# Down products with both weight parts as one moving operand of 512 columns, centred output weights, and one slot for both attention halves

## The reference

```python
def attention(h):                            # 8 heads of 32, norm_w of 32
    q, k, v = h @ Wq.T, h @ Wk.T, h @ Wv.T
    o = causal linear attention, in chunks of 64:
        inter = q @ state; intra = (q k^T * tril) @ v; state += k^T v
    denom = max(|sum(q * cumsum(k))|, 1)
    o = o / denom
    o = o * rsqrt(mean(o * o) + 1e-5) * norm_w
    return o @ Wo.T

def ffn(h):                                  # 8 experts, 256 -> 256 -> 256, all of them computed
    w = routing weights of 8 experts from sigmoid(h @ Wr / temperature)
    e_out = (silu(h @ Wg[e]) * (h @ Wu[e])) @ Wd[e]
    return sum over e of w[e] * e_out

x = x + _layernorm(attention(_layernorm(x)))
x = x + _layernorm(ffn(_layernorm(x)))
```

## Time and profile before

| | |
|---|---|
| median of 3 runs | 1494.8 us (1493.81 to 1496.97) |
| the profiled execution | 1496.2 us |
| its span | 1494.5 us |
| mean granted clock of PE | 0.995 of full |
| PE busy | 98% |
| DVE busy | 69% |
| ACT busy | 43% |
| POOL busy | 30% |
| DMA | 24.6 MB, 16 GB/s over the span |

### The profile page before, as it was taken

One profiled execution on the slowest core, in us unless ns is written; L12 is line 12 of the kernel. 1 busy time (PEld: TensorE's weight loads), 2 busy tenths in 40 slices (PEclk: granted clock), 3 DMA queues, 4 the chain that ended last, 5 costly groups with the idle time before them and its releaser, 6 DMA issues. The chain is left out here.

```text
span 1494.5 us, 37390 instructions
## 1 busy us (share of the span) xinstructions
PE 1465.5 (98%) x14438; PEld 1279.1 (86%) x14438; DVE 1023.8 (69%) x2492; ACT 647.2 (43%) x1189; POOL 442.9 (30%) x653
## 2 busy tenths in 40 slices
PE   7799999999999999999999999999999999999997
PEld 6688888888888888888888888888888888888886
DVE  6667667676776767667675776767667676776765
ACT  5443534445354443534445354443534445344333
POOL 1403414133251233414134141232413234141231
PEclk9899999999999999999999999999999999999999
DMA  5100000000000000000000000000000000000000
GB/s 171 57 2 15 15 0 14 14 14 14 0 18 10 14 14 9 19 0 14 14 14 14 0 14 14 14 14 0 28 0 14 14 14 14 0 14 16 2 8 22
DMA packets 25345, 24.59 MB, mean 16 GB/s; under 512 B 2016, under 2 KB 25056, under 8 KB 25312
## 3 DMA queue, kind: packets, MB, share of 16 engines
q1 hardware_dynamic: 25312, 24.13, 5.1%
HBM read 15.74 MB, written 8.39 MB: 16 GB/s over the span
## 5 line engine op out<-in xcount | busy, mean ns | idle before, releaser
L1002 DVE TENSOR_TENSOR late<-late,up_ps 128x512 f32<-128x512 f32 x256 | 174.9, 683 | 155.7 <-PE up_ps L436 99.1
L705 ACT ACTIVATE h_hi<-late 128x512 fp32r<-128x512 f32 x256 | 161.6, 631 | 247.2 <-DVE late L1002 247.2
L436 PE MATMUL down_ps<-w_hi,h_hi 128*128 128x256 f32 x976 | 264.5, 293 | 0.0
L786 ACT ACTIVATE late<-gate_ps 128x512 f32<-128x512 f32 x256 | 152.3, 595 | 252.1 <-PE gate_ps L436 252.1
L436 PE MATMUL down_ps<-w_hi,h_lo 128*128 128x256 f32 x976 | 254.1, 282 | 0.0
L1225 POOL TENSOR_TENSOR rms_in<-rms_in,minus_half 128x16 f32<-128x16 f32 x32 | 93.4, 2919 | 498.3 <-DVE rms_in L958 498.3
L899 DVE TENSOR_TENSOR h_lo<-late,h_hi 128x512 fp32r<-128x512 f32 x256 | 175.7, 686 | 65.0 <-ACT h_hi L705 65.0
L1024 DVE SCALAR_TENSOR_TENSOR late<-down_ps,route,late 128x256 f32<-128x256 f32 x364 | 158.4, 477 | 87.9 <-PE down_ps L436 84.9
L436 PE MATMUL gate_ps<-ft_hi,w_hi 128*128 128x512 f32 x512 | 204.9, 400 | 1.0 <-ACT ft_hi L705 0.8
L436 PE MATMUL gate_ps<-ft_hi,w_lo 128*128 128x512 f32 x512 | 203.5, 397 | 0.0
L436 PE MATMUL up_ps<-ft_hi,w_hi 128*128 128x512 f32 x512 | 199.7, 390 | 0.0
(11 more groups left out here) (170 smaller groups left out, 2481.9 us busy)
## 6 DMA issues: line engine op xcount, KB each, us to landing
xs<-in_x SPq DMA_DIRECT2D x32, 256.0 KB, 2.9
out_rows<-late SPq DMA_DIRECT2D x32, 256.0 KB, 2.2
late<-in_wg SPq DMA_DIRECT2D x7, 256.0 KB, 4.1
late<-in_wu SPq DMA_DIRECT2D x7, 256.0 KB, 4.4
late<-in_wd SPq DMA_DIRECT2D x6, 256.0 KB, 4.2
late<-in_wkv_t SPq DMA_DIRECT2D x1, 512.0 KB, 3.9
x<-in_wd SPq DMA_DIRECT2D x2, 256.0 KB, 4.6
late<-in_wq_t SPq DMA_DIRECT2D x1, 256.0 KB, 4.6
```

Of the source, the lines that this page charges most:

```text
L436: last = nc.tensor.matmul(dst, lhs, rhs, start=n == 0, stop=n == len(terms + low_terms) - 1)
L705: return nc.scalar.activation(dst, src, ACT.Copy)
L786: nc.scalar.activation(h_f[:, m, :], gate_ps[:, :], ACT.Silu).then_inc(silu_ready[0], 1)
L1002: nc.vector.tensor_tensor(h_f[:, m, :], h_f[:, m, :], up_ps[m][:, :], ALU.mult).then_inc(h_ready[0], 1)
```

## The change

What is computed stays the same up to the order of sums.

1. **Down products.** `w_hi` and `w_lo` become two halves of one tensor `w_parts`. A tile of `h_hi` meets both parts of the down weights in one matmul of 512 moving columns; the result has high-part products in columns 0 to 255 and low-part products in 256 to 511. A tile of `h_lo` meets the high part only, into columns 0 to 255. Each token tile now has a bank of its own (`down_ps` has two), and `acc` has 512 columns a tile. `add_down` adds all 512; for expert 7 a further `tensor_tensor` adds the two halves into `fin`. ACT's copy of expert 0's product and its scaling by the route are twice as long too.
2. **One up bank.** `up_ps` is one bank, so `up(e, m)` waits for the `hidden` just before it, not for the one before that.
3. **Centred output weights.** In the first block each row of the scaled `wo` has its mean subtracted, so the wo product has mean zero. ACT's copy to `rows` and DVE's centring go; DVE takes the moments straight out of PSUM, and `ln2_add` reads PSUM.
4. **Slots.** Both halves of `ot`, of `wo` and of `ln2_stats` stand together, and all of that stands later (below). The normalisation of half 1 before `ft` goes from ACT to DVE (`ln3_norm`), and `ft` waits for both halves before it begins.
5. **State updates.** Two `scalar_tensor_tensor` on all 128 partitions, masked by `odd_even`, in place of four `tensor_tensor` on 32 partitions, for each of four chunks; the state is laid out anew.
6. **Memory and start.** Half 1 of `kz` lies in `x1` (ACT then waits for `x1_copied`), `late` grows from 3072 to 4096 columns, so that no weight unit is staged in `x1`, and the first block's lists are ordered a little differently.
7. **End.** DVE centres the last pair, and multiplies and adds it itself, without ACT.

The rows that follow are the order of instructions, word for word, as the two programs issue them; they hold no times. First DVE in the last pass of `rest`, experts 6 and 7, before: `late<-down_ps` is `add_down`, `late<-late,up_ps` is `hidden`, `x<-...` is `ln2_add` (x is x1), `h_lo` is `low_hidden`.

The diff, cut to its core:

```diff
-    [("ot", 0)],
+    [],
     [("norm_apply", 1), ("carry",)],
-    [("wo", 0), ("ot", 1)],
-    [("ln2_stats", 0)],
-    [("wo", 1), ("ln2_add", 0)],
-    [("ln2_stats", 1)],
-    [("ln3_stats", 0)],
-    [("ln2_add", 1), ("ln3_stats", 1)],
-    [("ln3_apply", 0)],
-    [("ln3_apply", 1)],
+    [("ot", 0), ("ot", 1)],
+    [],
+    [("wo", 0), ("wo", 1)],
+    [("ln2_stats", 0), ("ln2_stats", 1)],
+    [("ln2_add", 0)],
+    [("ln2_add", 1), ("ln3_stats", 0)],
+    [("ln3_stats", 1)],
+    [("ln3_apply", 0), ("ln3_norm", 1)],
...
-        w_hi = sb("w_hi", [P, 3 * E, 2, 256], f32r)
-        w_lo = sb("w_lo", [P, 3 * E, 2, 256], f32r)
+
+        w_parts = sb("w_parts", [P, 2, 3 * E, 2, 256], f32r)
+        w_hi, w_lo = w_parts[:, 0, :, :, :], w_parts[:, 1, :, :, :]
...
-        up_ps = [bank(f"up_ps{m}") for m in range(MT)]
-        down_ps = bank("down_ps")
+        up_ps = bank("up_ps")
+        down_ps = ctx.enter_context(nc.psum_tensor("down_ps", [P, 2, 512], f32))
...
-                reach(pe, h_ready, f, 2 * e + m - 1)
-                into(up_ps[m], 1).then_inc(up_done[0], 1)
+                reach(pe, h_ready, f, 2 * e + m)
+                into(up_ps, 1).then_inc(up_done[0], 1)
...
                 dst = down_bank(e, p, f)
                 for t in range(2):
                     c = slice((2 * p + t) * P, (2 * p + t) * P + P)
-                    last = products(dst[:, t * HID:t * HID + HID],
-                                    [((h_hi[:, e % 2, m, c], h_lo[:, e % 2, m, c]),
-                                      (w_hi[:, 3 * e + 2, m, :], w_lo[:, 3 * e + 2, m, :])) for m in range(MT)])
+                    for m in range(MT):
+                        nc.tensor.matmul(dst[:, t, :], h_hi[:, e % 2, m, c], w_parts[:, :, 3 * e + 2, m, :],
+                                         start=m == 0, stop=False)
+                        last = nc.tensor.matmul(dst[:, t, 0:HID], h_lo[:, e % 2, m, c], w_hi[:, 3 * e + 2, m, :],
+                                                start=False, stop=m == MT - 1)
...
-                    reach(pe, x1n_ready, a, p + 1)
+                    reach(pe, x1n_ready, a, p + 1 if is_first(a) else 2)
...
+                    if step[1] == 1:
+                        reach(act, x1_copied, a, 0)
...
-                elif kind == "wo":
-                    p = step[1]
-                    copy(rows[:, 2 * p:2 * p + 2, :], src)\
-                        .then_inc(wo_copied[0], 1)
...
-                        added = att_half(step, a)[:, i, :].rearrange("p (b g y v) -> p b g y v", b=B, g=HG, y=2)
-                        for j in range(HPG):
-                            x, y = divmod(j, 2)
-                            rows_j = slice(D * j, D * j + D)
-                            before_i, after_i = (state[rows_j, :, m, :, y * VA:(y + 1) * VA] for m in (n + i, n + i + 1))
-                            last = nc.vector.tensor_tensor(after_i, before_i, added[rows_j, :, :, y, :], ALU.add)
+                        added = att_half(step, a)[:, i, :].rearrange("p (n y v) -> p n y v", n=B * HG, y=2)
+                        for y in range(2):
+                            before_i, after_i = (state[:, m, :, :, y * VA:(y + 1) * VA]
+                                                 .rearrange("p b g v -> p (b g) v") for m in (n + i, n + i + 1))
+                            last = nc.vector.scalar_tensor_tensor(after_i, added[:, :, y, :], odd_even[:, y:y + 1], before_i,
+                                                                  ALU.mult, ALU.add)
...
                 elif kind == "ln2_stats":
                     p = step[1]
-                    reach(dve, wo_copied, a, p + 1)
-                    ln_stats(2, rows, range(2 * p, 2 * p + 2), bn2, mv2)
-                    reach(dve, moments_ready[1], a, p + 1)
-
+                    reach(dve, att_done, a, number_of(("wo", p), a) + 1)
+                    for b in range(B):
+                        last = nc.vector.bn_stats(bn2[:, 2 * p + b, :], att_half(("wo", p), a)[:, b, :])
+                    settle(last)
                     for t in range(2 * p, 2 * p + 2):
-                        last = nc.vector.tensor_scalar(rows[:, t, :], rows[:, t, :], mv2[:, t, 0:1], None, ALU.subtract)
-                    last.then_inc(centred[0], 1)
+                        last = nc.vector.bn_aggr(mv2[:, t, :], bn2[:, t, :])
+                    last.then_inc(moments_ready[1][0], 1)
                 elif kind == "ln2_add":
                     p = step[1]
                     reach(dve, rstd_ready[1], a, p + 1)
-                    reach(dve, centred, a, p + 1)
                     reach(dve, x1_copied, a, 0)
-                    for t in range(2 * p, 2 * p + 2):
-                        last = nc.vector.scalar_tensor_tensor(x1[:, t, :], rows[:, t, :], rstd2[:, t:t + 1], xs[:, t, :],
-                                                              ALU.mult, ALU.add)
+
+                    for b in range(B):
+                        t = 2 * p + b
+                        last = nc.vector.scalar_tensor_tensor(x1[:, t, :], att_half(("wo", p), a)[:, b, :], rstd2[:, t:t + 1],
+                                                              xs[:, t, :], ALU.mult, ALU.add)
                     last.then_inc(x1_ready[0], 1)
                 elif kind == "ln3_stats":
                     p = step[1]
                     reach(dve, x1_ready, a, p + 1)
                     ln_stats(3, x1, range(2 * p, 2 * p + 2), bn3, mv3)
+                elif kind == "ln3_norm":
+                    p = step[1]
+                    reach(dve, rstd_ready[2], a, p + 1)
+                    reach(dve, moments_ready[2], a, p + 1)
+                    for t in range(2 * p, 2 * p + 2):
+                        last = nc.vector.tensor_scalar(rows[:, t, :], x1[:, t, :], mv3[:, t, 0:1], rstd3[:, t:t + 1],
+                                                       ALU.subtract, ALU.mult)
+                    last.then_inc(x1n_ready[0], 1)
...
-                    t, src = 2 * p + n, down_bank(e, p, f)[:, n * HID:(n + 1) * HID]
-                    dst = fin if e == E - 1 else acc
-                    last = nc.vector.scalar_tensor_tensor(dst[:, t, :], src, route[:, t, e:e + 1], acc[:, t, :],
-                                                          ALU.mult, ALU.add)
+                    t = 2 * p + n
+                    last = nc.vector.scalar_tensor_tensor(acc[:, t, :], down_bank(e, p, f)[:, n, :], route[:, t, e:e + 1],
+                                                          acc[:, t, :], ALU.mult, ALU.add)
+                if e == E - 1:
+                    settle(last)
+                    ts = slice(2 * p, 2 * p + 2)
+                    last = nc.vector.tensor_tensor(fin[:, ts, :], acc[:, ts, 0:HID], acc[:, ts, HID:2 * HID], ALU.add)
...
+                    for g in range(HG):
+                        last = nc.vector.bn_stats(bn4[:, g, :], wo_raw[:, g, :])
+                    settle(last)
+                    for g in range(HG):
+                        last = nc.vector.bn_aggr(mv4[:, g, :], bn4[:, g, :])
+                    settle(last)
+                    for g in range(HG):
+                        last = nc.vector.tensor_scalar(wo_raw[:, g, :], wo_raw[:, g, :], mv4[:, g, 0:1], None, ALU.subtract)
                     last.then_inc(wo_scaled, 1)
...
+            dve.wait_ge(moments_ready[3][0], 2 * BLOCKS)
+            for t in range(2, 4):
+                last = nc.vector.tensor_scalar(fin[:, t, :], fin[:, t, :], mv4[:, t, 0:1], None, ALU.subtract)
+            settle(last)
+            out_add(nc.vector, dve, 0, f)
+            dve.wait_ge(x1_copied[0], BLOCKS)
+            dve.wait_ge(rstd_ready[3][0], 2 * BLOCKS)
+            for t in range(2, 4):
+                last = nc.vector.scalar_tensor_tensor(x1_kept[:, t, :], fin[:, t, :], rstd4[:, t:t + 1], x1_kept[:, t, :],
+                                                      ALU.mult, ALU.add)
+            last.then_inc(last_out_ready, 1)
 
```

92 lines of the change are left out of this document (46 added, 46 removed).

## The result

The changed kernel takes 1539.6 us (median of 4 runs, 1538.2 to 1542.0) against 1495.4 us before: 1.0297 times as long, 95% interval 1.028 to 1.0315. That is 44 us more; the forecast was 28 us more (1523, range 1508 to 1548). The profiled execution took 1539.0 us with a span of 1537.3, 42.8 us more than before.

What follows compares the result with a forecast made beforehand. PE's order of work was taken as the whole bound. 15 blocks at +2.84 - 0.34 - 0.58 = +1.92 us give +28.8; last block -0.6, ends -0.5: +27.7 on 1494.8, so 1523 us, range 1508 to 1548.

Steps and rivals of the forecast that it cites:

- rival 3: DVE's long additions cost two pairs: +0.75 us a block, 1534 us; chance 0.09 together with rival 4.
- rival 4: Down products: the two-piece moving operand saves nothing, 1532 us; chance 0.09 together with rival 3.
- rival 1: PE's clock also falls around `ft`: 1527 to 1538 us in some blocks, 1549 to 1574 in all; chance 0.17.
- The chain before `ft`: DVE's layer-norm chain makes PE stand 2.84 us a block: 0.8 before expert 6's down product, 2.0 before `ft`.
- POOL's way: Before `ft`: POOL's roots, then normalisation, end at 782.0 on the forecast's clock, together with DVE's way at 782.1.
- The down products: On PE, fewer, wider matmuls save 0.036 us a product, 0.58 us a block, 9.2 us in all.
- A turn: One turn of the loop takes 92.0 us after the change, against 90.1 before.
- The last block: Its products were to take 0.6 us less.
- Rival 5: The single up bank stops PE, `up` waiting for the hidden product; part of the same 2.8 us; no chance of its own.
- Start: First block: wo's copy and centring leave the chain to `ft`, about 1.5 us; with the end -0.5, bounds -4 and +3.
- End: Longer additions and joining the halves outlast the last ACT pass and its waits by about 1 us.

Runs made afterwards that it cites:

- last_block: Changed kernel with one DVE step moved in the last block: hidden product of expert 2, half 0, ahead of the routing weights and scaling; 1542.2 us in its one run.
- order_only: Kernel before with only the new step order in front of `ft`; short additions, centring and two up banks kept; 1530.4 us, ratio 1.0237.
- short_additions: Changed kernel with `add_down` over the first 256 of its 512 columns, low-part sum left out of the output; 1512.5 us, ratio 1.0118.
- one_piece: Changed kernel with the down products' 512-column moving operand taken from one piece, low-part products left out of the output; 1543.5 us in its one run.
- chain_early: Changed kernel, all operations kept, with the slots of the whole chain before `ft` moved earlier; 1506.2 us, ratio 1.0078.
- narrow_down: Kernel of old_order with each down product as 12 matmuls of 256 columns in place of 4 of 512 and 4 of 256; 1513.9 us, ratio 1.0112.
- old_order: Changed kernel with the old step order before `ft`, so with ACT's wo copies and ACT's normalisation of half 1 back; 1511.3 us, ratio 1.011.
- wo_slot_early: Changed kernel with only the start changed: high and low part of the output weights made before the first expert weights; 1542.1 us, ratio 1.0307.
- centred_swap: Kernel before with output weights centred once, no loop centring, and their scaling moved behind low wq and the second normalisation; 1494.7 us, ratio 0.9994.
- centred_warm: Kernel before with output weights centred once, no loop centring, their scaling later, and filler matmuls before `ft` and the first gate; 1497.9 us, ratio 1.0011.

## Why the prediction was right, and what it mis-sized

The direction, the place and the mechanism were right; the size was 16 us short. The standing of PE was sized well; the other large terms all missed to the same side. That the result still lies in the range is in part luck: the high end of 1548 stood for rivals 3, 4 and 1, and none of them came.

- *The chain before `ft`* (2.84 us of standing a block): 0.75 + 1.70 us idle, and 0.91 + 1.86 = 2.77 us when read from the start of one matmul to the next less a usual pitch. Its links (addition pair 1.33, low part 0.60, statistics 1.06) stood as laid. POOL's way, said to end together with DVE's, did not: its last root ended at 799.67 us, and `ln3_norm` began at 800.34, behind DVE's own work. DVE's order alone decided.
- *The down products* (0.58 us a block): this term was mis-sized. A down product that follows other matmuls without a pause takes 1.432 us before and 1.400 after, 0.032 us less and near the forecast's 0.036. But over all of them (239 in the loop of each) it is 1.478 and 1.460, 0.29 us a block. Products whose first matmul is slow in both kernels save less (1.527 to 1.513), and two of the sixteen have a slow first matmul (0.33 us in the place of 0.23) in the changed kernel alone; one of them is the product that waits for `h_lo`. Inside the down products a wide matmul takes 0.233 to 0.236 us, where the forecast took 0.2295 from gate and up products. The excess is 4 us over 15 blocks. The forecast's sentence that the rows give 0.012 us a matmul besides its columns was a wrong reading: its own two pitches give 2 x 0.119 - 0.2295 = 0.0085.
- *A turn*: 92.43 in the place of 92.0. Of the difference 0.28 us is the down products; 0.1 us is spread over gate, up and attention products and not explained.
- *First and last turn*: 1.9 us more than 15 turns of 2.31 us, though two waits for `issue` of 1.4 and 1.2 us stand there; the clock in the first turn of the kernel before hides a part. No step had them.
- *The last block* (-0.6): +1.8. Rival 5, the single up bank, was looked at in the loop alone, where it costs nothing; in the last block the next gate and up product follow the routing weights directly, and PE stood 2.7 us. last_block shows bank and DVE both in it; order_only, with two up banks, has no such wait.
- *Start* (-1.5, with bounds that reached +3 together with the end): +2.5. The wo copy and the centring did leave the chain: the changed kernel is 4.2 us behind at the first wo product (44.1 against 39.9) and 3.2 us at the first gate (60.95 against 57.76). But 2.3 us more of `issue` at 31.4 us, a kv product that waits 0.4 us longer, and 28 warm-up matmuls that took 6.15 in the place of 5.21 us (their pitch fell from 0.213 to 0.112 us at 10.0 in the place of 8.0 us), stand against it. Behind the `issue` stand the clock was at its half level from 33.9 to 37.3 us, which the kernel before has nowhere between 24 and 54 us. The first mark lies between 67.4 and 71.5 us over the runs of this start, and it follows the clock: 67.4 with 3.4 us at the half level between 10 us and the mark, 68.4 and 69.3 with 6.8, 69.6 with 10.2, 70.0 to 71.5 with 13.7. The forecast had no term for this.
- *End* (+1): +1.8, the right sign. With short additions it is +0.4 (short_additions, 10.0 us behind the last matmul against 9.6), so the length of the additions makes 1.4 of it. Start and end together are +4.3, outside the forecast's bounds of -4 and +3.
- *Rivals*: the clock did not fall in the loop (1.00 in every turn), not even behind 1.7 us of standing; it fell in the first block, as above. Additions at two pairs fall (1.32 us). The two-piece operand falls (one_piece).

The sum of what was mis-sized is 5.9 (turns), 1.9 (first and last), 4.0 (start), 2.4 (last block) and 0.8 us (end): 15.0, against 15.1 between 42.8 and 27.7.

## What to carry to other kernels

Where an engine's in-order queue alternates between feeding the busy engine and a dependent chain, the chain's end is set by the slots of its members, the last one above all, together with the lengths that stand behind the late slot. order_only against the kernel before, and chain_early against the changed one, move little but places, and each moves a turn by over 2.2 us; short_additions moves no place and takes 1.7 us off. What is removed from a chain helps only as far as the chain is what PE waits for. So a step that saves copies by making two products wait together is to be laid out in slots before it is counted as a gain. And a bank taken away is to be checked in every stretch of the program, the last block too, not only in the loop.

## What the runs showed of the hardware that was not expected

Fusing two 256-column matmuls into one of 512 saves 8 ns where the down product follows other matmuls without a pause (1.432 to 1.400 us for four fusions), and 6.6 ns in the mean of all down products (narrow_down against old_order). From start to start it is 117 to 120 ns at 256 columns and 233 to 236 ns at 512.

The first matmul behind a wait takes 0.10 us longer than the others of its kind until the next starts: 0.33 us at 512 columns in the place of 0.23 (795.11 to 795.44 in the changed kernel).

In the first block of twelve kernels, all but wo_slot_early and centred_swap, PE stood for "issue" (nothing that the profile shows) for 0.4 to 3.2 us at the same s product, among 64-column matmuls that start every 15 ns in the mean. The stretch around it in the changed kernel, one of the same in the kernel before, and SyncE's wait in the changed one:

```profile
28.00:30.00 2.00, 1.85 (x93) 1.58 (x82) 1.85 (x6) 1.40 (x3) 0.00 (x0) 1.00 0.98 343
30.00:32.00 2.00, 1.42 (x30) 1.15 (x30) 0.34 (x2) 1.44 (x4) 0.00 (x0) 1.00 1.12 377
...
34.00:36.00 2.00, 1.68 (x55) 1.58 (x54) 0.00 (x0) 0.47 (x1) 1.99 (x1) 0.50 0.06 17
```
```profile
30.00:32.00 2.00, 1.35 (x63) 1.21 (x58) 1.30 (x5) 2.00 (x4) 0.23 (x1) 1.00 0.33 110
...
34.00:36.00 2.00, 1.68 (x58) 1.34 (x51) 2.00 (x4) 0.03 (x1) 0.68 (x1) 1.00 0.00 0
```
```profile
SPq L421 <- DVE wo_lo L902: 8.6, 1, 8.6
```

SyncE waits 8.6 us for the staging slot of the output weights, and the loads behind it crowd into 24 to 33 us; the DMA share at 30 to 32 us is 1.12 against 0.33, the stand 2.90 against 0.65 us. Over the runs, the eight with a share over 1.0 at 30 to 32 us stood 2.2 to 3.2 us there, the four under 0.7 stood 0.4 to 1.6 us. In all eight the granted clock went to its half level at 31.7 to 35.0 us, during the stand or right behind it, and in none of the four. It looks like PE's program that comes late over the same DMA engines; that was argued from this pattern, and the two runs meant to show it moved PE as well. One more pattern speaks for it: in all twelve the stand ends 2.3 to 2.6 us after the start of a packet of DMA queue q8, which the profile calls `instruction` (31.83 and 34.32 us in the changed kernel, 28.41 and 30.75 before). That the stand waits for this packet is not shown. Like waits, 0.8 to 1.4 us, stood in the first and last turn of the kernels with wide down products, and not in narrow_down; but centred_warm, without wide products, has 0.6 and 1.1 us in its last turn, so the width alone does not decide it. Which property of the program does stays open.
